# A batch of eight images through pooling branches, depthwise convolutions and attention: borders of the stem's end and of the levels reordered on ScalarE and VectorE, and the box sums of products split into fp32r parts in twelve of 24 steps

## The chip, the cores and the metric

The kernel runs on one core of one Trainium2 chip. A core has five engines that run their own queues in order and meet through semaphores: TensorE (PE, with PEld for its weight loads), VectorE (DVE), ScalarE (ACT), GpSimd (POOL) and SyncE (SP, which issues the DMAs here). The metric is the device time of one execution in microseconds (us), lower is better, as a median of runs.

## The reference

`x` has 8 images of 256 channels and 32x32 pixels. What the change touches lies in the first half of the function, up to the concatenations:

```python
def _sumpool(x): return lax.reduce_window(x, 0.0, lax.add, WIN, (1, 1, 1, 1), PAD)      # 5x5
def _tmaxavg(x): return 0.9 * _maxpool(x) + 0.1 * (_sumpool(x) / 25)
def _rwpool(x):
    c = lax.stop_gradient(jnp.max(x))              # over the whole batch
    e = jnp.exp(x - c)
    return _sumpool(e * x) / (_sumpool(e) + 1e-06)

x_aux = _cbs(_gn(x), w_sta, b_sta)                 # 1x1 convolution to 128 channels, silu
y1, y2 = [x_aux], [x_aux]
for _ in range(3):
    y1.append(_tmaxavg(y1[-1]))
    y2.append(_rwpool(y2[-1]))
y = concat([_cbs(concat(y1), w_cv1, b_cv1), _cbs(concat(y2), w_cv2, b_cv2)])
a = c1(ddwv(ddwh(dwv(dwh(y)))))                    # four depthwise convolutions, one 1x1
x = x + _cbs(y * a, w_cvend, b_cvend)
x = x + attention(_gn(x), w1, w2)                  # 1024 tokens, softmax, per image
```

The maximum `c` of `_rwpool` runs over all eight images, so each of its three applications (a level) needs all images of the one before.

## The kernel before

There are three stages, one after the other, with a barrier of the engines between them: the stem (`phase_a`), the levels (`phase_b`) and the rest, image by image (`phase_c`). The change lies in the first two.

The stem normalises each image on VectorE (`normalise(n)`, two instructions that write `xn`), multiplies by `w_sta` on TensorE (`convolve(n)`), and applies silu on ScalarE (`silu(n)`, into `x_all[:, n, 0]`); VectorE then takes each row's maximum (`maximum(n)`, into `rmc`). ScalarE rounds weights to fp32r (`split`), GpSimd takes the rests (`low_parts`). Beside that, the chain of `_tmaxavg` for image 0 runs in its own tensors (`Chain`): image 0's stem output is loaded into `chain.wide[:, 0]` by a DMA; VectorE forms the 5x5 maximum in seven steps (`chain.maxima(dve, 0, level, steps)`: step 0 writes `pairs`, step 1 is a small copy of borders into `pairs`, 2 writes `work_a`, 3 `tall`, 4 `work_a`, 5 and 6 `work_b`); ScalarE copies the level into `zero` (`chain.zero_level`), and GpSimd forms the 5x5 sum from it in six adds (`chain.box_sum_step`); VectorE joins both into the next level (`chain.mixture_of_sums`). `box` is the 0/1 matrix of neighbouring pixels, rounded once to fp32r from `box_raw`. The orders of these instructions are written out by hand in the code of each engine.

The levels run `_rwpool`. There are 24 steps (`total = LEVELS * B`), numbered m or s: steps 0 to 7 are the images of the first level, 8 to 15 of the second, 16 to 23 of the third. For one step:

- TensorE transposes the image (`turn(m)`, into `ps_t`).
- ScalarE takes the exponential (`exponent(m)`, into `e`) and rounds it to fp32r (`e_hi`). GpSimd takes the rest (`e_low(m)`, `e_lo`). VectorE multiplies (`product(m)`, `ey = e * x`), which frees `ps_t`.
- TensorE sums over 5x5 windows by products with `box`, which also transpose back: `sum_e(m)` as two passes of fp32r matmuls, 10 with `e_hi` and 10 with `e_lo` (`box_sum`), and `sum_ey(m)` in fp32 (`box_sum_whole`), which appears in the trace as 20 matmuls.
- ScalarE forms 1/(sum + eps) by a logarithm and an exponential (`estimate(m)`); VectorE improves it (`residual`, `improve`, into `newton`) and multiplies with the sum of products (`divide(m)`), which gives `y(m)`, back in `x_all`, its row maximum in `rmc`, and frees `ps_ey`. A DMA stores `y(m)`.

At a level's start (s = 0, 8, 16) VectorE and TensorE form the maximum over the batch (`reduce_tile`, `spread_max`, `reduce_batch`), and ScalarE forms `eps` from it (`set_eps`), which `estimate` of that level needs.

In step s TensorE runs sum_ey(s), turn(s + 2), sum_e(s + 1). ScalarE runs estimate(s), exponent(s + 2), and at a level's start the exponent first, then set_eps and estimate. VectorE runs product(s + 1), residual(s), improve(s), divide(s), and then one step of the image 0 chain in some of them. GpSimd runs e_low(s + 2) and then one add of the chain in steps 0 to 5 and 9 to 14. `ps_ey` is a single buffer: sum_ey(s + 1) waits for y(s). `turn` waits for the product before it, since `ps_t` is single too.

## Time and profile before

| | us |
|---|---|
| median of 3 runs | 1458.1 |
| lowest and highest | 1456.68, 1458.79 |
| the profiled execution | 1458.25 |
| its span, first to last instruction | 1456.5 |
| stem, of the span | 0 to about 88.4 |
| levels, of the span | 88.7 to 286.6, then 2.8 for the last store |
| images (`phase_c`) | from 289.5 on |

A page of the profile gives busy times of the engines, the chain of work that ended last, and groups of instructions. The trace behind it gives each instruction with its start. A matmul's end is modelled. Idle time of an engine is shown before the instruction that ended it, with the one it was waiting for.

### The profile page before, as it was taken

The numbers are of one execution on the slowest core, as the hardware profiler recorded it, in microseconds if no ns is written. First come the engines' busy times: TensorE is split into PE (matmuls) and PEld (weight loads), VectorE is DVE, ScalarE is ACT, GpSimd is POOL, SyncE is SP. The second block draws the span as 40 slices with busy tenths as digits, with TensorE's granted clock in tenths as the row PEclk, the third lists the DMA queues.
The fourth block names the chain that finished last, engine by engine and source line by source line (L and its number), as shares of the span: only waits on it lengthen the run. The fifth ranks groups of instructions, "written<-read, shape, count | busy, mean of one in ns | idle before, by whom it ended". The sixth has DMA issues, their size and how long they took to land.

```text
span 1456.5 us, 18340 instructions
## 1 busy us (share of the span) xinstructions
PE 1292.0 (89%) x7162; PEld 1077.5 (74%) x7162; DVE 1143.7 (79%) x1218; ACT 691.9 (48%) x749; POOL 128.8 (9%) x64
## 2 busy tenths in 40 slices
PE   3649898872999999999999999999999999999797
PEld 1238797742768986888688878877986798688597
DVE  7858686678689887988798798879877998796443
ACT  0335564562246536543654365347435653564333
POOL 1645363200000000000000000000000000000000
PEclk9778998985999999999999999999999999999899
DMA  7401122210000020001002000200020002000000
GB/s 286 158 15 73 58 93 82 88 58 0 29 15 1 16 87 14 0 33 68 14 0 72 29 14 0 72 29 14 0 94 6 14 14 86 0 1 30 29 1 29
DMA packets 19175, 62.84 MB, mean 43 GB/s; under 512 B 1600, under 2 KB 4288, under 8 KB 19136
## 3 DMA queue, kind: packets, MB, share of 16 engines
q1 hardware_dynamic: 18432, 62.00, 11.4%
q8 instruction: 27, 0.44, 0.1%
q10 hardware_dynamic: 704, 0.30, 0.1%
q14 instruction: 12, 0.10, 0.0%
HBM read 36.61 MB, written 25.17 MB: 42 GB/s over the span
## 4 chain that ended last, share of the span: by engine, by line
PE 63%; issue 14%; DVE 12%; ACT 5%; DMA 0%; DVEq 0%; ACTq 0%; POOLq 0%; POOL 0%
PE slot L1094 21%; PE slot L1132 12%; PE ps_o L1132 9%; PE ps_ey L565 6%; DVE between L1407 4%; PE slot L549 3%; PE slot L1148 3%; PE ps_e L549 3%; DVE a L1407 2%; PE slot L1072 2%; PE ps_t L633 1%; PE slot L1119 1%; PE ps_ot L1164 1%; ACT f_all L1283 1%; PE slot L1055 1%
## 5 line engine op out<-in xcount | busy, mean ns | idle before, releaser
L1132 PE MATMUL slot<-f_all,q_all 128*128 128x512 f32 x768 | 196.9, 409 | 13.4 <-ACT pooled L1273 13.4
L1132 PE MATMUL ps_o<-v_all,pt_all 128*128 128x256 f32 x1536 | 199.2, 286 | 5.4 <-ACT mixed L1292 5.2
L1132 PEld LDWEIGHTS ps_o<-v_all,pt_all 128*128 128x128 f32 x1536 | 188.8, 192 | 7.6 <-DVE pt_all L1411 6.2
L1132 PEld LDWEIGHTS slot<-f_all,q_all 128*128 128x128 f32 x768 | 145.2, 195 | 43.9 <-ACT pooled L1273 14.8
L1407 DVE SCALAR_TENSOR_TENSOR a<-between,k_columns,a 128x992 f32<-128x992 f32 (+1 forms) x128 | 157.5, 1232 | 4.9 <-ACT a L1264 2.6
L1287 ACT CAST v_all<-y 128x1024 fp32r<-128x1024 f32 x32 | 33.7, 1052 | 185.8 <-DVE y L1438 185.8
L1411 DVE TENSOR_TENSOR pt_all<-slot,pt_all 128x1024 fp32r<-128x1024 f32 x64 | 78.2, 1222 | 47.5 <-ACT pt_all L1278 47.5
L1072 PE MATMUL slot<-wide,k_cv 128*128 128x512 f32 x256 | 114.3, 597 | 0.0
L565 PE MATMUL ps_ey<-box,x_all 128*128 128x192 f32 (+2 forms) x480 | 95.5, 358 | 19.6 <-DVE rmc L751 12.8
L565 PEld LDWEIGHTS ps_ey<-box,x_all 128*128 128x128 f32 x480 | 84.2, 204 | 26.3 <-issue 20.2
L1264 ACT ACTIVATE a<-between,k_columns 128x1024 f32<-128x1024 f32 x64 | 79.5, 1242 | 48.7 <-DVE between L1407 47.7
L1292 ACT ACTIVATE mixed<-ps_o,row_inv 128x256 f32<-128x256 f32 x64 | 30.1, 471 | 151.8 <-PE ps_o L1132 151.8
L1024 POOL TENSOR_TENSOR c_rstd<-c_spread,k_minus_half 128x2 f32<-128x2 f32 x8 | 5.6, 698 | 1093.2 <-DVE gmean L1477 1093.2
L1416 DVE TENSOR_REDUCE c_minus_max<-slot 128x1 f32<-128x1024 f32 x64 | 78.1, 1220 | 11.2 <-PE slot L1132 11.2
L1072 PEld LDWEIGHTS slot<-wide,k_cv 128*128 128x128 f32 x256 | 47.5, 190 | 51.4 <-issue 50.7
L1407 DVE SCALAR_TENSOR_TENSOR between<-y,k_columns,between 128x992 f32<-128x992 f32 x64 | 79.4, 1250 | 7.0 <-ACT between L1264 5.9
L1278 ACT CAST pt_all<-slot 128x1024 fp32r<-128x1024 f32 x64 | 65.0, 1015 | 37.3 <-PE slot L1148 37.1
L1273 ACT ACTIVATE pooled<-slot,c_minus_max 128x1024 f32<-128x1024 f32 x64 | 71.6, 1119 | 21.5 <-DVE c_minus_max L1416 21.5
L1438 DVE SCALAR_TENSOR_TENSOR y<-slot,k_columns,y 128x1024 f32<-128x1024 f32 x32 | 41.0, 1281 | 51.2 <-PE slot L1094 35.0
L1407 DVE SCALAR_TENSOR_TENSOR between<-a,k_columns,between 128x960 f32<-128x960 f32 x64 | 77.2, 1215 | 1.1
L1257 ACT ACTIVATE y<-slot,k_columns 128x1024 f32<-128x1024 f32 x32 | 35.4, 1105 | 81.0 <-PE slot L1094 81.0
L1148 PE MATMUL slot<-k_ident,pooled 128*128 128x128 f32 x512 | 66.8, 273 | 4.0 <-ACT pooled L1273 4.0
(160 smaller groups left out, 2649.3 us busy)
## 6 DMA issues: line engine op xcount, KB each, us to landing
levels<-x_all SPq DMA_DIRECT2D x32, 512.0 KB, 2.6
x_all<-in_x SPq DMA_DIRECT2D x8, 1024.0 KB, 13.2
q_all<-levels SPq DMA_DIRECT2D x8, 1024.0 KB, 4.9
x<-in_x SPq DMA_DIRECT2D x8, 1024.0 KB, 4.8
out<-x SPq DMA_DIRECT2D x8, 1024.0 KB, 3.9
pooled<-levels SPq DMA_DIRECT2D x8, 512.0 KB, 3.3
wide<-levels SPq DMA_DIRECT2D x7, 512.0 KB, 3.3
x_all<-in_w_c SPq DMA_DIRECT2D x2, 512.0 KB, 3.6
```

The lines of the kernel that those rows point to most:

```text
L549: last = nc.tensor.matmul(out[:, r0 * W:r1 * W], part[:, k * P:(k + 1) * P], box[:, c0:c0 + (r1 - r0) * W], start=(b not in started), stop ...
L565: last = nc.tensor.matmul(out[:, r0 * W:r1 * W], whole[:, k * P:(k + 1) * P], box[:, c0:c0 + (r1 - r0) * W].bitcast(F32), start=(b not in ...
L1072: last = nc.tensor.matmul(slot[:, h * HALF:(h + 1) * HALF], keep["cv1"][:, k, cols(m)], rows, start=(k == 0), stop=(k == KT - 1))
L1094: last = nc.tensor.matmul(slot[:, hs], weights[:, k], inputs(k)[:, hs], start=(at == 0), stop=(at == len(uses) - 1))
L1132: last = nc.tensor.matmul(out, lhs, rhs, start=(n == 0), stop=(n == len(parts) - 1))
L1148: last = nc.tensor.transpose(slot[:, cols(m)], prob[:, cols(m)], keep["ident"][:, :])
L1264: nc.scalar.activation(dst, src, ACT.Identity, scale=keep["taps"][:, s, c, 1:2], bias=keep["b_taps"][:, s, c:c + 1]).then_inc(taps_centre. ...
L1273: nc.scalar.activation(prob[:, :], slots_of["s", t][:, :], ACT.Exp, bias=minus_max[:, t:t + 1], accum_out=row_sum[:, t:t + 1]).then_inc(pr ...
L1278: nc.scalar.copy(pt_hi[:, t % 2], slots_of["t", t][:, :]).then_inc(pt_hi_done.sem, 1)
L1407: nc.vector.scalar_tensor_tensor(o, u, keep["taps"][:, s, c, tap:tap + 1], o, ALU.mult, ALU.add).then_inc(taps.sem, 1)
L1411: nc.vector.tensor_tensor(pt_lo[:, t % 2], slots_of["t", t][:, :], pt_hi[:, t % 2].bitcast(F32), ALU.subtract).then_inc(pt_lo_done.sem, 1)
L1416: nc.vector.tensor_reduce(minus_max[:, t:t + 1], slots_of["s", t][:, :], AX, ALU.max, negate=True).then_inc(maxed.sem, 1)
```

## The change

On ScalarE the stem's end runs silu(7), then the rounding of `box` (which VectorE did), and then the copy of level 1 into `zero`; before, that copy, which waits for VectorE's mixture, stood ahead of silu(7).

On VectorE the stem's end runs steps 0 and 1 of the first maxima before maximum(1), normalise(n) before maximum(n - 3), and no step of level 1's maxima; those all move into the levels.

In the levels the sums of products are split: for all steps m outside `WHOLE` (so for 0, 7 to 10 and 17 to 23, twelve steps) ScalarE rounds `ey` to `ey_hi`, GpSimd forms `ey_lo`, and sum_ey is two passes of fp32r matmuls. In 1 to 6 and 11 to 16 it stays fp32. GpSimd's adds for level 2 start one step later (10 to 15); its adds then stand in the steps s in which it forms no `ey_lo`. At a level's start ScalarE runs set_eps and estimate before the exponent. VectorE runs level 1's maxima in steps 0 to 6 (its mixture in 8, before 7) and level 2's in 9 to 14 and 17. The copy of level 2 into `zero` moves from step 8 to 9.

```diff
@@ -403,8 +403,10 @@
             split("c1")
             silu(6)
             split("cv2")
+            silu(7)
+            act.wait_ge(box_in, 16)
+            nc.scalar.copy(box[:, :], box_raw[:, :]).then_inc(box_ready, 1)
             chain.zero_next(act, 1)
-            silu(7)
 
         @block.tensor
         def _(pe):
@@ -519,18 +521,16 @@
             maximum(0)
             shifts(1)
             normalise(group)
+            chain.maxima(dve, 0, 0, 0, 1)
             maximum(1)
-            first_maxima = ((0, 1, 2), (3, 4), (5, 6))
+            between = ((2, 3), (4,), (5, 6))
             for n in range(group + 1, B):
+                normalise(n)
                 maximum(n - 3)
-                normalise(n)
-                chain.maxima(dve, 0, 0, *first_maxima[n - group - 1])
-            dve.wait_ge(box_in, 16)
-            nc.vector.tensor_copy(box[:, :], box_raw[:, :]).then_inc(box_ready, 1)
+                chain.maxima(dve, 0, 0, *between[n - group - 1])
             maximum(B - 3)
             chain.mixture_of_sums(dve, 0)
             maximum(B - 2)
-            chain.maxima(dve, 0, 1, 0, 1, 2)
             maximum(B - 1)
 
 
@@ -569,6 +569,9 @@
     return last
 
 
+WHOLE = frozenset([*range(1, 7), *range(11, 17)])
+
+
 def phase_b(nc, keep, levels, x_all, rmc, box, chain, pooled):
 
 
@@ -585,6 +588,8 @@
         newton = x_all[:, 6, 1]
         e_hi = sb("e_hi", [P, 2, N], F32R)
         e_lo = sb("e_lo", [P, 2, N], F32R)
+        ey_hi = sb("ey_hi", [P, 2, N], F32R)
+        ey_lo = sb("ey_lo", [P, 2, N], F32R)
         tile_max = sb("tile_max", [P, LEVELS])
         batch_max = sb("batch_max", [P, LEVELS])
         minus_max = sb("minus_max", [P, 1])
@@ -596,7 +601,7 @@
 
         turned = sem("turned")
         exp_done, e_hi_done, e_lo_done = sem("exp_done"), sem("e_hi_done"), sem("e_lo_done")
-        ey_done = sem("ey_done")
+        ey_done, ey_hi_done, ey_lo_done = sem("ey_done"), sem("ey_hi_done"), sem("ey_lo_done")
         sum_e_done, sum_ey_done = sem("sum_e_done"), sem("sum_ey_done")
         log_done, r_done = sem("log_done"), sem("r_done")
         residual_done, newton_done, y_done = sem("residual_done"), sem("newton_done"), sem("y_done")
@@ -604,6 +609,10 @@
         shifts_done, eps_set = sem("shifts_done"), sem("eps_set")
         stored = pooled.stored
         block = ctx.enter_context(nc.Block())
+
+        def splits(m):
+
+            return len([k for k in range(m) if k not in WHOLE])
 
         def level_starts(s):
 
@@ -640,10 +649,17 @@
                 box_sum(nc, pe, box, ps_e[:, m % 2], e_hi[:, m % 2], e_lo[:, m % 2], (e_lo_done, m + 1)).then_inc(sum_e_done, 1)
 
             def sum_ey(m):
-                pe.wait_ge(ey_done, m + 1)
+                if m in WHOLE:
+                    pe.wait_ge(ey_done, m + 1)
+                else:
+                    pe.wait_ge(ey_hi_done, splits(m) + 1)
                 if m:
                     pe.wait_ge(y_done, m)
-                box_sum_whole(nc, pe, box, ps_ey, ey[m % 2]).then_inc(sum_ey_done, 1)
+                if m in WHOLE:
+                    last = box_sum_whole(nc, pe, box, ps_ey, ey[m % 2])
+                else:
+                    last = box_sum(nc, pe, box, ps_ey, ey_hi[:, m % 2], ey_lo[:, m % 2], (ey_lo_done, splits(m) + 1))
+                last.then_inc(sum_ey_done, 1)
 
             def spread_max(level):
 
@@ -676,6 +692,12 @@
                 act.wait_ge(exp_done, m + 1)
                 nc.scalar.copy(e_hi[:, u], e[u]).then_inc(e_hi_done, 1)
 
+            def product_hi(m):
+                act.wait_ge(ey_done, m + 1)
+                if m > 1:
+                    act.wait_ge(sum_ey_done, m - 1)
+                nc.scalar.copy(ey_hi[:, m % 2], ey[m % 2]).then_inc(ey_hi_done, 1)
+
             def estimate(m):
                 u = m % 2
                 act.wait_ge(sum_e_done, m + 1)
@@ -698,12 +720,14 @@
                 first = level_starts(s)
                 if s >= 0 and not first:
                     estimate(s)
-                if s + 2 < total:
-                    exponent(s + 2)
+                if 0 <= s + 1 < total and s + 1 not in WHOLE:
+                    product_hi(s + 1)
                 if first:
                     set_eps(s // B)
                     estimate(s)
-                if s == 8:
+                if s + 2 < total:
+                    exponent(s + 2)
+                if s == 9:
                     chain.zero_next(act, 2)
 
         @block.gpsimd
@@ -713,10 +737,17 @@
                 pool.wait_ge(e_hi_done, m + 1)
                 nc.gpsimd.tensor_tensor(e_lo[:, u], e[u], e_hi[:, u].bitcast(F32), ALU.subtract).then_inc(e_lo_done, 1)
 
+            def product_low(m):
+                u = m % 2
+                pool.wait_ge(ey_hi_done, splits(m) + 1)
+                nc.gpsimd.tensor_tensor(ey_lo[:, u], ey[u], ey_hi[:, u].bitcast(F32), ALU.subtract).then_inc(ey_lo_done, 1)
+
             for s in range(-2, total):
+                if 0 <= s + 1 < total and s + 1 not in WHOLE:
+                    product_low(s + 1)
                 if s + 2 < total:
                     e_low(s + 2)
-                for level, begin in ((1, 0), (2, 9)):
+                for level, begin in ((1, 0), (2, 10)):
                     if begin <= s < begin + 6:
                         chain.box_sum_step(pool, 0, level, s - begin)
 
@@ -777,13 +808,14 @@
                     residual(s)
                     improve(s)
                     divide(s)
-                if 0 <= s < 4:
-                    chain.maxima(dve, 0, 1, s + 3)
-                if s == 7:
+                if 0 <= s < 7:
+                    chain.maxima(dve, 0, 1, s)
+                if s == 8:
                     chain.mixture_of_sums(dve, 1)
-                if 9 <= s < 9 + MIX - 1:
+                if 9 <= s < 15:
                     chain.maxima(dve, 0, 2, s - 9)
                 if s == 17:
+                    chain.maxima(dve, 0, 2, 6)
                     chain.mixture_of_sums(dve, 2)
 
 
```

On ScalarE, around step 8, where the second level starts, before: L675 and L677 are the exponent and its rounding, L691 `eps`, L684 and L686 the estimate.

```order
L684 ACTIVATE x_all<-ps_e,eps 128x1024 [waits b_newton_done,b_sum_e_done]
L686 ACTIVATE x_all<-x_all 128x1024 [waits b_log_done]
L675 ACTIVATE x_all<-ps_t,minus_max 128x1024 [waits b_sum_e_done,b_e_lo_done,b_turned]
L677 CAST e_hi<-x_all 128x1024 [waits b_exp_done]
L675 ACTIVATE x_all<-ps_t,minus_max 128x1024 [waits b_sum_e_done,b_e_lo_done,b_turned]
L677 CAST e_hi<-x_all 128x1024 [waits b_exp_done]
L691 ACTIVATE eps<-batch_max,eps_shift 128x1 [waits b_batch_max_done]
L684 ACTIVATE x_all<-ps_e,eps 128x1024 [waits b_newton_done,b_sum_e_done,b_eps_set]
L686 ACTIVATE x_all<-x_all 128x1024 [waits b_log_done]
```

The same place in the changed kernel (L706 and L708 are the estimate, L691 and L693 the exponent, L713 `eps`, L699 the rounding of the product):

```order
L706 ACTIVATE x_all<-ps_e,eps 128x1024 [waits b_newton_done,b_sum_e_done]
L708 ACTIVATE x_all<-x_all 128x1024 [waits b_log_done]
L699 CAST ey_hi<-x_all 128x1024 [waits b_sum_ey_done,b_ey_done]
L691 ACTIVATE x_all<-ps_t,minus_max 128x1024 [waits b_sum_e_done,b_e_lo_done,b_turned]
L693 CAST e_hi<-x_all 128x1024 [waits b_exp_done]
L699 CAST ey_hi<-x_all 128x1024 [waits b_sum_ey_done,b_ey_done]
L713 ACTIVATE eps<-batch_max,eps_shift 128x1 [waits b_batch_max_done]
L706 ACTIVATE x_all<-ps_e,eps 128x1024 [waits b_newton_done,b_sum_e_done,b_eps_set]
L708 ACTIVATE x_all<-x_all 128x1024 [waits b_log_done]
L691 ACTIVATE x_all<-ps_t,minus_max 128x1024 [waits b_sum_e_done,b_e_lo_done,b_turned]
L693 CAST e_hi<-x_all 128x1024 [waits b_exp_done]
```

The exponent of step 10 has moved behind `eps` and the estimate of step 8, and two roundings of `ey` have come in.

On VectorE, step 0 of the levels, before (L735 residual, L742 improve, L751 divide, L730 product):

```order
L735 SCALAR_TENSOR_TENSOR ps_e<-ps_e,eps,x_all 128x1024 [waits b_r_done]
L742 SCALAR_TENSOR_TENSOR x_all<-ps_e,x_all 128x1024 [waits b_residual_done]
L751 ISA x_all,rmc<-x_all,ps_ey 128x1024 [waits stored0,b_sum_ey_done,b_newton_done]
L751 ISA rmc 128x1
L224 TENSOR_TENSOR tall<-work_a,pairs 128x1024 [waits chain_done]
L730 TENSOR_TENSOR x_all<-ps_t,x_all 128x1024 [waits b_sum_ey_done,b_exp_done]
```

and in the changed kernel, with the chain's piece of the next step:

```order
L782 ISA x_all,rmc<-x_all,ps_ey 128x1024 [waits stored0,b_sum_ey_done,b_newton_done]
L782 ISA rmc 128x1
L224 TENSOR_TENSOR pairs<-wide 128x32x31 [waits chain_loaded]
L761 TENSOR_TENSOR x_all<-ps_t,x_all 128x1024 [waits b_sum_ey_done,b_exp_done]
L766 SCALAR_TENSOR_TENSOR ps_e<-ps_e,eps,x_all 128x1024 [waits b_r_done]
L773 SCALAR_TENSOR_TENSOR x_all<-ps_e,x_all 128x1024 [waits b_y_done,b_residual_done]
L782 ISA x_all,rmc<-x_all,ps_ey 128x1024 [waits stored1,b_sum_ey_done,b_newton_done]
L782 ISA rmc 128x1
L203 COPY pairs<-wide 128x32x2
```

Level 1's first three maxima steps, which stood in the stem, now stand behind the divides of steps 0 to 2, and the others three steps later than before.

## Rows read from the trace of the kernel before

**Rows 1.** The page's first line.

```profile
span 1456.5 us, 18340 instructions
```

**Rows 2.** By stretches: busy us (instructions) of PE, PEld, DVE, ACT, POOL; PE clock, DMA, GB/s.

```profile
112.00:119.00 7.00, 6.97 (x25) 6.33 (x26) 4.78 (x5) 0.00 (x0) 0.00 (x0) 0.57 0.18 75
119.00:162.00 43.00, 42.62 (x314) 41.06 (x311) 34.74 (x36) 28.22 (x26) 26.63 (x12) 1.00 0.19 75
290.00:1457.00 1167.00, 1080.38 (x5932) 896.93 (x5932) 936.08 (x989) 567.34 (x629) 5.58 (x8) 0.97 0.08 27
```

**Rows 3.** The chain that ended last, step 6 of the levels: start, us, what.

```profile
148.35 3.50 PE ps_ey L565 x20
151.84 0.87 PE ps_t L633 x8
152.72 2.28 PE ps_e L549 x20
```

**Rows 4.** Timeline of the second level's start: start us, us, engine, line, what [idle before].

```profile
163.46 0.28 DVE L761 TENSOR_REDUCE batch_max<-ps_e 128x1 f32<-128x128 f32 x1
167.33 1.11 ACT L675 ACTIVATE x_all<-ps_t,minus_max 128x1024 f32<-128x1024 f32 x1 [5.74 <-PE ps_t L633]
168.48 1.05 ACT L677 CAST e_hi<-x_all 128x1024 fp32r<-128x1024 f32 x1
169.43 0.29 ACT L691 ACTIVATE eps<-batch_max,eps_shift 128x1 f32<-128x1 f32 x1
169.75 1.11 ACT L684 ACTIVATE x_all<-ps_e,eps 128x1024 f32<-128x1024 f32 x1
175.95 5.43 PE L565 MATMUL ps_ey<-box,x_all 128*128 128x192 f32 x20 [6.38 <-DVE rmc L751]
```

**Rows 5.** Timeline of the first level's start.

```profile
98.84 3.66 PE L565 MATMUL ps_ey<-box,x_all 128*128 128x192 f32 x20
105.69 2.35 POOL L714 TENSOR_TENSOR e_lo<-x_all,e_hi 128x1024 fp32r<-128x1024 f32 x1 [5.09 <-ACT e_hi L677]
108.07 1.29 DVE L735 SCALAR_TENSOR_TENSOR ps_e<-ps_e,eps,x_all 128x1024 f32<-128x1024 f32 x1 [9.72 <-ACT x_all L686]
112.03 6.64 PE L565 MATMUL ps_ey<-box,x_all 128*128 128x192 f32 x20 [6.40 <-DVE rmc L751]
```

**Rows 6.** Timeline, sum_ey of steps 7, 11, 17 and 19, and the last divide.

```profile
154.82 3.66 PE L565 MATMUL ps_ey<-box,x_all 128*128 128x192 f32 x20
...
190.99 3.66 PE L565 MATMUL ps_ey<-box,x_all 128*128 128x192 f32 x20
...
238.52 6.54 PE L565 MATMUL ps_ey<-box,x_all 128*128 128x192 f32 x20 [6.38 <-DVE x_all L754]
...
254.68 3.66 PE L565 MATMUL ps_ey<-box,x_all 128*128 128x192 f32 x20
...
285.36 1.22 DVE L754 SCALAR_TENSOR_TENSOR x_all<-x_all,ps_ey 128x1024 f32<-128x1024 f32 x1
```

**Rows 7.** Timeline of the stem's end, VectorE and GpSimd.

```profile
47.07 1.54 DVE L499 TENSOR_SCALAR xn<-x_all,rstd,shift 128x1024 f32<-128x1024 f32 x2 [0.55 <-PE ps_a L424]
49.71 1.19 DVE L224 TENSOR_TENSOR pairs<-wide 128x992 f32<-128x992 f32 x1 [1.10 <-DMA wide<-x_all]
...
58.58 2.81 POOL L187 TENSOR_TENSOR sum_a<-tall_sum 128x1088 f32<-128x1088 f32 x1
58.97 3.50 DVE L224 TENSOR_TENSOR tall<-work_a,pairs 128x1024 f32<-128x1024 f32 x1
...
75.66 4.58 DVE L529 CAST box<-box_raw 128x256 fp32r<-128x256 f32 x1
80.06 2.39 POOL L454 TENSOR_TENSOR k_cv_lo<-x_all,k_cv_hi 128x1024 fp32r<-128x1024 f32 x1
...
87.19 1.21 DVE L504 TENSOR_REDUCE rmc<-x_all 128x1 f32<-128x1024 f32 x1
```

**Rows 8.** Timeline, the border copy of level 2's maxima in step 10.

```profile
190.52 0.22 DVE L203 COPY pairs<-wide 128x64 f32<-128x64 f32 x1
```

## Prediction, before the changed kernel ran

> **What bounds the kernel now.** I read the span and the busy times by stretches first [rows 1, 2]. In the levels TensorE is busy nearly all the time between 119 and 162 us at full clock, GpSimd two thirds of it; the images from 290 us on take 1167 us and the change touches nothing there. So the change lives in the first 289 us. Then I read the chain that ended last, for a step in the middle of a level [rows 3]: it runs through TensorE alone, 3.50 us of sum_ey, 0.87 of turn, 2.28 of sum_e, 6.65 us a step. At a level's start it leaves TensorE: the timeline shows the batch maximum ready at 163.74, yet ScalarE forms `eps` at 169.43, since it first waits for the transpose of step 10 and runs exponent and rounding (1.11 and 1.05); the estimate starts at 169.75, and TensorE, idle for 6.38 us, starts sum_ey(9) at 175.95 [rows 4]. The same stands at step 1 and at step 17 [rows 5, 6]. From the estimate's start to the next sum_ey it is 175.95 - 169.75 = 6.20 us; I call this the y path. After such an idle time TensorE's clock reads 0.57 for 7 us, near its 1.2 GHz level, and sum_ey takes 6.64 in place of 3.5 [rows 2, 5].
>
> **A split step.** sum_e shows what two fp32r passes cost: 2.28. So a split sum_ey is 2.28 for 3.50, and TensorE's step 2.28 + 0.87 + 2.28 = 5.43. But sum_ey(n+1) also needs y(n), one y path after sum_e(n) ends, and sum_e(n) ends when sum_ey(n) could start at the earliest, 5.43 after sum_ey(n-1) started. Two steps are thus at least 6.20 + 5.43 = 11.6, or 5.8 a step. The split is worth 0.85 a step, not 1.22. ScalarE has five passes of about 1.1 in it (5.4), GpSimd two of 2.35 (4.7) [rows 2, 4, 5]: both fit.
>
> **GpSimd and VectorE exclude each other.** In the stem VectorE's maxima step starts at 58.97, 0.4 after a GpSimd add that ends at 61.39, and ends at 62.47, 1.1 after that end, where such a step alone takes 1.2 [rows 7]. The rounding of `box` started at 75.66 takes 4.58, to just past 80.06, where GpSimd's next instruction starts. So a VectorE instruction with both inputs in SBUF that finds GpSimd at work waits for that instruction's end. In the levels before, none of them met one: the chain's step came just ahead of e_low. When it meets one, product, residual, improve and divide behind it are late.
>
> **The levels, followed through.** I write A(n) for the start of sum_ey(n). A(0) = 98.84 stays.
> - Level 1. `eps` no longer waits for the exponent of step 2, so the estimate starts at 98.9 and A(1) = 105.1, for 112.03 before [rows 5]; the idle time shrinks from 6.4 to under 1 us, and sum_ey(1) runs at full clock. e_low(2) starts at 104.2 (98.84 + 2.28 + 0.87 + 1.15 + 1.05) and ends at 106.6. The maxima step behind divide(0), issued at 105.0, waits for it and ends at 107.7. Product(2) 1.14 more; from a residual's start to the next sum_ey it is 112.03 - 108.07 = 3.96 [rows 5]: A(2) = 112.8. The next chain step is the border copy, 0.22 [rows 8]; if it doesn't wait, y(2) is early again and the rest is TensorE's pace: A(7) = 112.8 + 5 x 6.65 = 146.0, for 154.82 [rows 6]: 8.8 gained.
> - Step 7 gives only half: the last maxima step meets the first `ey_lo` of the level on GpSimd, so A(8) = 153.3.
> - Second start. The batch maximum comes at 154.2, the rounding of the product and `eps` lie in front, the estimate starts at 155.1, A(9) = 161.3, for 175.95: 14.6 gained. The mixture, now in step 8, waits for e_low(10) to 161.7; it ends at 162.8, product 163.9, A(10) = 167.9. The first maxima step of level 2 waits for e_low(11) to 169.9: A(11) = 176.1, for 190.99 [rows 6]: 14.9. Five whole steps and 0.5 for the batch maximum: A(16) = 209.8.
> - Third start: the estimate at 211.3, A(17) = 217.5, for 238.52: 21.0. A(18) = 222.9. In step 17 the last maxima step and the mixture both stand on VectorE, and the mixture waits for e_low(19) to 225.8: 226.9, 228.0, A(19) = 232.0, for 254.68: 22.7.
> - Then 5.8 a step: A(22) = 249.4, sum_e(23) ends at 254.0 (no turn there), and one y path less 0.14 later y(23) at 260.0, for 285.36 + 1.22 = 286.58 [rows 6]: **26.6 gained**. The last store and the start of the images follow it as before.
>
> The 26.6 by cause, roughly: the three starts 6.9, 5.1 and 5.4, the clock that no longer falls there 3.1, 1.8 and 2.9, twelve splits 10, and some 8 to 9 lost again in waits for GpSimd.
>
> **The stem's end, worked at about nothing.** Off VectorE go the rounding of `box` and level 1's first three maxima steps (1.2 + 0.2 + 1.2). Against it, step 0 of level 0's maxima now stands ahead of maximum(1) and normalise(5) and waits for a DMA that lands at 49.7; normalise(5), done at 48.61 before, comes at 52.1 and meets GpSimd twice, to about 56.0 [rows 7]. GpSimd works from 50.9 to 82.45 without a gap, and VectorE's instructions with two inputs take turns with it, so GpSimd's end sets VectorE's: about 82, then the last maxima step, maximum(5), the mixture, maximum(6), maximum(7), 5 x 1.15 and a rest, 88.6 for 88.40. I take +0.2. Bounds: -1, if VectorE is through before GpSimd's last; +2.2, if one instruction more finds GpSimd's long one of 4.5. silu(7) and `box` on ScalarE hide under this.
>
> **Sum.** 1458.25 - 26.6 + 0.2 = 1431.9 against the profiled execution, which lies 0.15 above the median; rounded, **1431.7 us**.
>
> **A rule beside a row.** The border copy of 0.22 has never met GpSimd in the rows of before; the forecast lets it pass. The Trainium skill (SBUF — State Buffer, Who interferes with whom) says that a copy between SBUF tensors can enter a mode that uses the port shared with GpSimd, and then fully waits. No run here shows it for this copy. If so, it speaks for the first rival below.
>
> **Rivals.**
> - *A standing collision.* If the copy, or a shift of 0.5 us, leaves y(n) later than the end of sum_e(n+1), each maxima step meets e_low again, and the lateness feeds itself: a whole step is then e_low 2.35 + maxima 1.1 + product 1.2 + turn 0.87 + sum_e 2.28 = 7.8, for 6.65. Four or five steps in a level, some 5 us: 1437 with one level, 1442 with both. For it: y(1) comes only 0.5 us behind e_low(3)'s start. Against: a copy of 0.22 has room, and TensorE's pace lets y catch up.
> - *The gain at the starts comes back.* The idle times of 2.7 us at step 9 and 3 at step 18 let the clock fall for several us as it did at step 1 (3.1 lost each time), or GpSimd, with 2 x 2.35 and a wait for VectorE, becomes late in split steps, 0.5 each in twelve: 1437 to 1440.
> - *Slower than before.* In split steps TensorE idles 0.4 of 5.8, again and again; if that alone kept it at the lower clock, a step would be about twice 5.4. That is over 5 us a step, and from the sixth such step on the 26.6 are gone; with all twelve, 1470. Against: from 290 us on TensorE is busy for 1080 of 1167 us, 93%, at a granted 0.97 [rows 2].
> - *The stem longer by more than the bound*, through another turn with GpSimd, gives 1434 at +2.2: inside the forecast's range.
>
> **How the numbers follow.** The forecast 0.64 (1428 to 1435: splits at TensorE's own 5.43 would give 1428), the standing collision 0.18, the gain given back 0.12, slower 0.04, and the rest, that both gains cancel, 0.02. The range takes in the forecast and one level and more of collision: 1427 to 1441. A measurement of this kernel tells 0.2%, 2.9 us, from no change. Faster by over that 0.94, the same 0.02, slower 0.04.
>
> **What would show it.** sum_ey(1) 6 to 7 us after sum_ey(0), at a granted clock near 1.00; `eps` ahead of the exponent at 155; split steps 5.8 apart from step 19 on, with TensorE idle for 0.3 to 0.4 on VectorE's y; one long maxima instruction in step 0, at 8, 9 and 17, and none in 2 to 5 and 11 to 14; the border copy at 0.22 and not over 1. Wrong if whole steps are 7.8 apart, if the clock falls at steps 9 or 19, or if the levels start after 91.

## The result, and the profile after

| | before | changed |
|---|---|---|
| median, us | 1458.55 (6 runs, 1456.68 to 1459.97) | 1434.04 (6 runs, 1429.68 to 1436.08) |
| the profiled execution, its span | 1458.25, 1456.5 | 1429.68, 1427.9 |
| levels start (`tile_max`), last `y(23)` ends | 88.72, 286.58 | 87.43, 260.22 |
| first product of the images, from there to the end | 290.71, 1165.8 | 264.30, 1163.6 |

The ratio is 0.983, with an interval of 0.981 to 0.985: 24.5 us less. The forecast was 26.6 - 0.2 less, 1431.7, with a range of 1427 to 1441. The profiled execution happens to be the shortest of the changed kernel's six. In the two profiled executions the levels take 172.8 us in place of 197.9, 25.1 less; the other 3.5 lie ahead of the levels (1.3) and in the images (2.2), whose code the change leaves alone.

The page of the changed kernel, its first line and the granted clock in 40 slices. A slice is 35.7 us; the levels lie in slices 3 to 8.

```profile
span 1427.9 us, 18374 instructions
...
PEclk9879999867999999999999999999999999999899
```

By stretches: the stretch's length, then busy us (instructions) of PE, PEld, DVE, ACT, POOL, then TensorE's granted clock, the DMA engines' share and GB/s.

```profile
98.00:146.00 48.00, 46.44 (x341) 44.35 (x340) 43.50 (x41) 31.72 (x30) 33.95 (x14) 1.00 0.17 69
...
160.00:167.00 7.00, 5.95 (x29) 5.98 (x29) 6.90 (x7) 2.25 (x3) 3.50 (x2) 0.58 0.19 77
167.00:218.00 51.00, 48.57 (x360) 46.86 (x358) 42.11 (x44) 35.79 (x35) 35.13 (x16) 0.99 0.21 83
218.00:223.00 5.00, 4.77 (x29) 4.80 (x29) 4.56 (x5) 2.09 (x2) 3.75 (x2) 0.66 0.27 108
223.00:255.00 32.00, 29.19 (x254) 28.72 (x252) 26.83 (x23) 27.54 (x27) 23.96 (x10) 1.00 0.30 115
```

The first level, which had a stretch at 0.57 [rows 2], now runs at 1.00 from end to end. The clock still falls behind the two later starts, to 0.58 and 0.66. The timeline of the first start (start us, us, engine, line, what, [idle before <- what ended it]):

```profile
97.55 1.31 PE L549 MATMUL ps_ey<-box,ey_hi 128*128 128x192 f32 x10
103.19 2.36 POOL L738 TENSOR_TENSOR e_lo<-x_all,e_hi 128x1024 fp32r<-128x1024 f32 x1 [3.62 <-ACT e_hi L693]
103.79 2.81 DVE L224 TENSOR_TENSOR pairs<-wide 128x992 f32<-128x992 f32 x1
104.01 3.71 PE L565 MATMUL ps_ey<-box,x_all 128*128 128x192 f32 x20 [0.88 <-DVE rmc L782]
...
111.19 2.35 POOL L738 TENSOR_TENSOR e_lo<-x_all,e_hi 128x1024 fp32r<-128x1024 f32 x1 [2.74 <-ACT e_hi L693]
111.37 2.26 DVE L203 COPY pairs<-wide 128x64 f32<-128x64 f32 x1
```

sum_ey(1) comes 6.46 us behind sum_ey(0), where it was 13.19 [rows 5], and TensorE's idle time before it went from 6.40 to 0.88. One maxima step, at 103.79, meets `e_lo` and takes 2.81. And the border copy, at 111.37, takes 2.26 where it took 0.22 [rows 8]: it began 0.18 us after GpSimd's instruction and ended when that had.

The second level's start:

```profile
153.45 0.28 DVE L792 TENSOR_REDUCE batch_max<-ps_e 128x1 f32<-128x128 f32 x1
154.53 0.29 ACT L713 ACTIVATE eps<-batch_max,eps_shift 128x1 f32<-128x1 f32 x1
154.85 1.11 ACT L706 ACTIVATE x_all<-ps_e,eps 128x1024 f32<-128x1024 f32 x1
156.96 1.10 ACT L691 ACTIVATE x_all<-ps_t,minus_max 128x1024 f32<-128x1024 f32 x1
161.05 2.38 PE L549 MATMUL ps_ey<-box,ey_hi 128*128 128x192 f32 x10 [2.71 <-DVE rmc L782]
163.22 2.33 PE L549 MATMUL ps_ey<-box,ey_lo 128*128 128x192 f32 x10
```

`eps` now follows the batch maximum by 1.1 us in place of 6.0 [rows 4], and stands ahead of the exponent. TensorE idles 2.71 us for 6.38, and the two passes behind it run at the lower clock, 2.4 and 2.3 in place of 1.3 each.

The split steps of the third level, and the end:

```profile
225.30 1.31 PE L549 MATMUL ps_ey<-box,ey_hi 128*128 128x192 f32 x10
...
231.69 1.36 PE L549 MATMUL ps_ey<-box,ey_hi 128*128 128x192 f32 x10 [0.80 <-DVE x_all L785]
...
237.17 1.31 PE L549 MATMUL ps_ey<-box,ey_hi 128*128 128x192 f32 x10
...
243.57 1.36 PE L549 MATMUL ps_ey<-box,ey_hi 128*128 128x192 f32 x10 [0.81 <-DVE x_all L785]
...
259.00 1.22 DVE L785 SCALAR_TENSOR_TENSOR x_all<-x_all,ps_ey 128x1024 f32<-128x1024 f32 x1 [0.38 <-PE ps_ey L549]
```

They come 5.48 and 6.40 apart by turns, 5.94 in the mean: every second one waits 0.8 us for y.

### The profile page after: what moved, and what is told of

Same layout as the page of the kernel before. It is cut to its first block, busy times and chain, and to the rows that moved or that the text cites. A ratio compares the mean times of both kernels' runs of the same rounds, so it can differ in the third digit from the quotient of the medians.

```text
span 1427.9 us, 18374 instructions
## 1 busy us (share of the span) xinstructions
PE 1273.4 (89%) x7162; PEld 1063.4 (74%) x7162; DVE 1148.8 (80%) x1217; ACT 704.6 (49%) x762; POOL 159.5 (11%) x76
## 4 chain that ended last, share of the span: by engine, by line
PE 59%; issue 14%; DVE 14%; ACT 6%; DMA 0%; DVEq 0%; ACTq 0%; POOLq 0%; POOL 0%
PE slot L1126 21%; PE slot L1164 12%; PE ps_o L1164 9%; DVE between L1439 5%; PE slot L549 3%; PE slot L1180 3%; DVE a L1439 2%; PE slot L1104 2%; PE ps_e L549 2%; PE ps_ey L565 2%; PE slot L1151 1%; PE ps_ey L549 1%; DVE ps_e L766 1%; DVE x_all L773 1%; PE ps_t L642 1%
## 5 line engine op out<-in xcount | busy, mean ns | idle before, releaser
L1296 ACT ACTIVATE a<-between,k_columns 128x1024 f32<-128x1024 f32 x64 | 79.4, 1241 | 48.6 <-DVE between L1439 47.7
L738 POOL TENSOR_TENSOR e_lo<-x_all,e_hi 128x1024 fp32r<-128x1024 f32 x24 | 61.5, 2563 | 47.6 <-ACT e_hi L693 47.6
L1126 PE MATMUL slot<-f_all,k_c_hi 128*128 128x512 f32 x232 | 64.0, 397 | 2.5 <-DVE y L1470 2.5
```

Of the source, the lines that this page charges most:

```text
L738: nc.gpsimd.tensor_tensor(e_lo[:, u], e[u], e_hi[:, u].bitcast(F32), ALU.subtract).then_inc(e_lo_done, 1)
L1126: last = nc.tensor.matmul(slot[:, hs], weights[:, k], inputs(k)[:, hs], start=(at == 0), stop=(at == len(uses) - 1))
L1296: nc.scalar.activation(dst, src, ACT.Identity, scale=keep["taps"][:, s, c, 1:2], bias=keep["b_taps"][:, s, c:c + 1]).then_inc(taps_centre. ...
```

## Experiments

The theory after this result: nearly all of the gain is ScalarE's new order at the three starts, with those falls of the clock that it avoids. The splits and the moved chain nearly cancel, since each place where the chain meets GpSimd costs what some two splits give. The rival: the parts give what the forecast's sum put down for each, above all 10 us for twelve splits. Each run below stands beside runs of the kernel before on the same chip; the medians of those were 1458.76 to 1458.97. "Levels" is from `tile_max` to the end of `y(23)` in the profiled execution, "images" from the first product behind it to the end of the span.

| kernel | median (lowest, highest) | ratio, interval | levels | images |
|---|---|---|---|---|
| before | 1458.55 (1456.68, 1459.97) | | 197.9 | 1165.8 |
| changed | 1434.04 (1429.68, 1436.08) | 0.983, 0.981 to 0.985 | 172.8 | 1163.6 |
| e1_again | 1433.90 (1431.58, 1439.19) | 0.983, 0.981 to 0.984 | 175.9 | 1168.6 |
| e2_no_split | 1435.62 (1432.99, 1436.68) | 0.984, 0.982 to 0.985 | 173.7 | 1167.2 |
| e3_splits_only | 1455.68 (1451.00, 1461.56) | 0.998, 0.997 to 1.000 | 194.9 | 1164.9 |
| e4_tail | 1435.45 (1435.07, 1438.07) | 0.985, 0.983 to 0.986 | 172.7 | 1167.7 |
| e5_act_order | 1436.49 (1431.40, 1437.74) | 0.984, 0.982 to 0.985 | 175.2 | 1167.4 |
| e6_border_reduce | 1433.64 (1432.82, 1441.62) | 0.984, 0.982 to 0.987 | 172.9 | 1164.9 |
| e7_placed_a | 1425.14 (1424.34, 1426.96) | 0.977, 0.976 to 0.978 | 163.5 | 1167.0 |
| e8_placed_b | 1428.43 (1428.08, 1428.56) | 0.979, 0.978 to 0.980 | 164.7 | 1168.7 |
| e9_old_stem | 1435.92 (1430.51, 1441.38) | 0.984, 0.982 to 0.986 | 173.7 | 1163.8 |
| e10_placed_whole | 1432.96 (1430.84, 1437.16) | 0.983, 0.980 to 0.985 | 171.1 | 1165.6 |

**e1_again**, the changed kernel once more, no edit.

> The changed kernel again, unaltered, for a second profile and more times: its six times spread over 6.4 us, those of before over 3.3. Theory A (clock): the waits for y at steps 9, 17 and 23 let TensorE's clock fall in some executions and not in others; the levels then end between 257 and 263 us after the span's start, whole steps stay 6.6 apart, and where the end is late a granted clock near 0.6 stands behind one of those waits. Theory B (standing collision): in slow executions the maxima steps of level 1 or 2 meet e_low again and again, whole steps are 7.8 apart, and several maxima rows take over 2 us. Time 1430 to 1437.

The median is the same, but the profiled execution, the longest of its five, is 9.5 us longer: 3.1 in the levels, 5.0 in the images, 1.2 before the levels. Theory A had the late end come with a fall of the clock. It was the other way round: the levels end at 264.5, beyond Theory A's 263, in the execution in which the clock at step 17 did not fall. So `e_lo` came early enough to meet the mixture, which in the first execution it had missed (there the last maxima step at 223.22 and the mixture at 224.55 took 1.22 each). Timeline of step 17:

```profile
225.15 2.39 POOL L738 TENSOR_TENSOR e_lo<-x_all,e_hi 128x1024 fp32r<-128x1024 f32 x1 [1.16 <-ACT e_hi L693]
225.40 3.22 DVE L230 SCALAR_TENSOR_TENSOR wide<-sum_b,work_b 128x1024 f32<-128x1024 f32 x1
...
230.03 1.06 PE L642 MATMUL ps_t<-k_ident,x_all 128*128 128x128 f32 x8 [2.65 <-DVE x_all L761]
...
234.86 2.33 PE L549 MATMUL ps_ey<-box,ey_hi 128*128 128x192 f32 x10
```

The mixture takes 3.22, TensorE idles 2.65 and then has the lower clock; sum_ey(19) starts 9.9 us behind sum_ey(18) where it was 6.4. Whole steps stay 6.63 apart in both executions, so there is no standing collision. The images differ mostly in the last one. From its `f_all` (ScalarE's first rounding of `pooled` for it) to the end the stretches read, first of the changed kernel's first profile, then of this one,

```profile
1201.42:1427.90 226.48, 203.52 (x1174) 172.91 (x1172) 138.16 (x162) 102.65 (x121) 1.39 (x2) 0.98 0.04 16
```

```profile
1206.89:1437.40 230.51, 207.56 (x1174) 176.74 (x1172) 138.28 (x162) 102.65 (x121) 1.39 (x2) 0.95 0.04 16
```

The same 1174 matmuls take 226.5 us at a granted 0.98 and 230.5 at 0.95. The other 1.0 us of the images lies ahead of them.

**e2_no_split**, the changed kernel with every sum of products in fp32:

```diff
-WHOLE = frozenset([*range(1, 7), *range(11, 17)])
+WHOLE = frozenset(range(24))
```

> All of the change except the splits: sum_ey is fp32 in all 24 steps; the orders of ScalarE and VectorE and the later chain stay. By the recurrence of the prediction with this kernel's order: the starts gain as before, steps go at 6.65, the mixture and maxima steps meet e_low as in the changed kernel: the levels end 24 us earlier than before, 1434 to 1436, about 3 us over the changed kernel. Rival (splits carry their 10 us in full on top of the orders): 1441 or more.

1.6 us more than the changed kernel, within both runs' scatter, and not 10. By levels, from the traces: first level (sum_ey(0) to sum_ey(8)) 53.3 us against 55.1 with the splits, second 57.4 against 57.3, third (to the end of `y(23)`) 52.7 against 50.2. So in these two executions the splits gain 2.5 us in the third level and lose 1.8 in the first; e1's third level, with its collision, took 53.2, and there they gain nothing. In step 0 a split cannot help, since y(0) waits for the estimate anyway; but it brings `e_lo` of step 2 forward by 1.2 us, into the chain's first maxima step. Without it that step took 1.19 and the border copy behind it 0.23. In the second level the chain's instructions of steps 8 to 10 met `e_lo` in whole steps too (3.02, 3.30 and 2.33). The mixture's new place does that: in e5 below, with whole steps and the mixture still in step 7, the same three took 1.22, 1.19 and 0.22.

**e3_splits_only**, the kernel before with the twelve splits and nothing else (of the edit, `WHOLE` and ScalarE's order; the rest of the splits' code is as in the change):

```diff
+WHOLE = frozenset([*range(1, 7), *range(11, 17)])
...
-                if s + 2 < total:
-                    exponent(s + 2)
+                if 0 <= s + 1 < total and s + 1 not in WHOLE:
+                    product_hi(s + 1)
+                if s + 2 < total:
+                    exponent(s + 2)
                 if first:
                     set_eps(s // B)
                     estimate(s)
```

> The kernel before with the twelve splits alone: stem, level starts on ScalarE (exponent ahead of eps) and VectorE's chain as before. If the splits are worth 0.85 each and the y path (6.2) is the limit of a split step: the levels end about 12 us earlier, 1446, split steps 5.8 to 6.2 apart, idle times of 6 us at steps 1, 9 and 17 stay, with the clock falling behind them. If splits are worth 1.22 each: 1443 or less. If they are worth nothing alone, 1456 or more.

A miss: 3.3 us gained against the kernel before on the same chip. The mixture of level 1 stood behind step 7's divide, and with step 7 split it met `e_lo`. Timeline:

```profile
159.71 2.33 POOL L738 TENSOR_TENSOR e_lo<-x_all,e_hi 128x1024 fp32r<-128x1024 f32 x1
160.11 3.02 DVE L230 SCALAR_TENSOR_TENSOR wide<-sum_b,work_b 128x1024 f32<-128x1024 f32 x1
163.17 0.16 DVE L788 TENSOR_REDUCE tile_max<-rmc 128x1 f32<-128x8 f32 x1
163.38 0.69 PE L667 MATMUL ps_e<-k_ident,tile_max 128*128 128x128 f32 x2 [3.85 <-DVE tile_max L788]
...
177.25 2.42 PE L549 MATMUL ps_ey<-box,ey_hi 128*128 128x192 f32 x10 [6.40 <-DVE rmc L782]
```

The mixture's 3.02 holds `tile_max` back and TensorE idles 3.85 there, with a granted clock of 0.66 over the 5 us behind it, ahead of the old 6.40 which stays. The level's two splits were eaten at its end: it took 64.6 us for 63.9 before. The second level, with three splits, took 63.1 for 62.6; its border copy met `e_lo` (1.93). Only the third, whose seven splits meet no instruction of the chain but the mixture, at 1.22, gained: 56.0 for 61.2, 0.7 us a split.

**e4_tail**, the changed kernel with the last maxima step and the mixture of level 2 behind the last divide:

```diff
-                if s == 17:
+                if s == total - 1:
                     chain.maxima(dve, 0, 2, 6)
                     chain.mixture_of_sums(dve, 2)
```

> The changed kernel with the last maxima step and the mixture of level 2 moved from step 17 behind the last divide (step 23). In step 17 they cost the wait for GpSimd and two instructions, 3 us by the prediction's recurrence, and behind the last divide VectorE is idle while the last store lands (2.8 us), so they should cost nothing there: 3 us less than the changed kernel, sum_ey(19) 6 us after sum_ey(18) in place of 8.6 to 9.1. Rival: the time comes back because the end of the levels waits for VectorE (2.4 us of work, ends within 0.5 us of the store): no gain or 0.5.

No gain in the median. In the profiled execution the clock fell at step 17 (the two passes of sum_ey(17) took 1.46 and 2.33), as in the changed kernel's first profile, and sum_ey(19) comes 6.4 us after sum_ey(18) in both: where the clock falls there was no collision to take away, and the levels are as long, 172.7 against 172.8. The two instructions behind the last divide end 2.5 us after it, at 263.7, yet the images' first product comes 4.4 us behind `y(23)`, for 4.1 to 4.4 in the kernels without them: they are nearly hidden. Whether an execution in which the clock stays up would be 3 us shorter than e1's levels stays open; none was profiled. The rest of the median is the images' 1167.7.

**e5_act_order**, the kernel before with ScalarE's order at a level's start alone:

```diff
-                if s + 2 < total:
-                    exponent(s + 2)
                 if first:
                     set_eps(s // B)
                     estimate(s)
+                if s + 2 < total:
+                    exponent(s + 2)
```

> The kernel before with one part of the change alone: at the two places where a level begins, ScalarE takes set_eps, the logarithm and the reciprocal before the exponential and copy of the step after next. The pooling chain, the whole-product sums (all 24) and the stem stay as before. Theory A: this order is nearly the whole gain. TensorE's idle 6.40 us at the two starts goes, the clock stays up behind it, and steps 8 and 16 to 17 come 7.9 and 7.3 us apart: sum_ey(1) at 105.2, sum_ey(9) at 160.3, sum_ey(17) at 215.3, the end of y(23) at 260.4, levels 171.8 long against 197.9 before; median 1431 to 1437 us. Theory B: the chain of before, whose last maximum and mixture stand at steps 3 and 7, meets the earlier start (as the splits alone did, where the mixture held the first divide of the level back), so half of the gain is lost: an idle of over 3 us of TensorE at one of the starts, levels of 180 to 186 us, median 1442 to 1448.

This swap gives 22.3 of the changed kernel's 24.5 us, and the intervals of the two overlap. It is 0.9 us over e2, which has the swap, the new stem and the moved chain: within both runs' scatter. The levels took 175.2 us, 3.4 over Theory A's 171.8; some 2 of it lie at the first start, where sum_ey(0) itself ran at a granted 0.63 (98 to 104 us) and sum_ey(1) came 8.27 behind it. The old chain did not get in the way:

```profile
153.42 1.22 DVE L230 SCALAR_TENSOR_TENSOR wide<-sum_b,work_b 128x1024 f32<-128x1024 f32 x1
154.10 2.75 POOL L714 TENSOR_TENSOR e_lo<-x_all,e_hi 128x1024 fp32r<-128x1024 f32 x1 [4.27 <-ACT e_hi L677]
...
156.21 0.29 ACT L691 ACTIVATE eps<-batch_max,eps_shift 128x1 f32<-128x1 f32 x1 [2.19 <-DVE batch_max L761]
```

In whole steps the chain's instruction starts 0.7 us ahead of `e_lo` and runs free, as it did before. The idle time before sum_ey(9) is 0.75, and from 104 to 225 us the granted clock reads 1.00. It reads 1.00 there in e2 and e10 too, the other kernels with the swap and without splits; in the seven profiles with the swap and splits it reads 0.96 to 0.99.

**e6_border_reduce**, the changed kernel with the 64 border elements written by another instruction:

```diff
-                own.did(self.nc.vector.tensor_copy(pairs[:, :, 1:W + 2:W], src[:, :, 0:W:W - 1]))
+                own.did(self.nc.vector.reduce_max(pairs[:, :, 1:W + 2:W],
+                        src[:, :, 0:W:W - 1].rearrange("p h (w o) -> p h w o", o=1), AX))
```

> The changed kernel with the pooling chain's border columns (64 elements) written by a reduction over an axis of length 1 in the place of the copy. Theory A: the copy waited for GpSimd (2.26 and 1.50 us where it had taken 0.22) because of the form of the instruction, a copy between SBUF tensors; a reduction with one input does not wait: 0.2 to 0.3 us at steps 1 and 10, whatever GpSimd runs. Theory B: whatever reads and writes SBUF at that moment waits: 1.4 to 2.3 us again. On the whole kernel both give the changed kernel's time within 1.5 us by A (one wait of up to 2.0 us is gone at step 1, where sum_ey(2) came 7.6 behind sum_ey(1), so at most 1 us of it shows at each of two steps): 1431.5 to 1434.5.

```profile
113.04 2.36 POOL L738 TENSOR_TENSOR e_lo<-x_all,e_hi 128x1024 fp32r<-128x1024 f32 x1 [2.73 <-ACT e_hi L693]
...
113.22 0.27 DVE L203 TENSOR_REDUCE pairs<-wide 128x64 f32<-128x64 f32 x1
```

At the same place, 0.18 us behind GpSimd's start, the reduction takes 0.27; the copy took 2.26. Over its 24 places it took 0.26 to 0.27. The Trainium skill (SBUF — State Buffer, "Who interferes with whom") says that a copy can enter a mode in which it needs the pair of ports shared with GpSimd and waits in full for GpSimd to finish, and that on this chip a reduction never contends; both halves agree with these rows, 2.26 and 0.27. The kernel's time does not show it: the step behind it was sum_ey(3), only 0.4 us late with the copy.

**e7_placed_a** and **e8_placed_b**, the changed kernel with the chain placed step by step. The places come from carrying the forecast's recurrence (each start of a sum worked out from those before it) through all 24 steps for many placements. A pair (level, k) is maxima step k, 7 the mixture; EARLY is ahead of the step's residual, LATE behind its divide. The edit of e7, in part:

```diff
-WHOLE = frozenset([*range(1, 7), *range(11, 17)])
+WHOLE = frozenset([4, 5, 6, 7, 8, 10, 16, 17])
+EARLY = {0: ((1, 0),), 1: ((1, 1),), 8: ((1, 7),), 16: ((2, 3),), 23: ((2, 6),)}
+LATE = {1: ((1, 2),), 3: ((1, 3),), 4: ((1, 4),), 5: ((1, 5),), 6: ((1, 6),), 9: ((2, 0),),
+        10: ((2, 1), (2, 2)), 19: ((2, 4),), 21: ((2, 5),), 23: ((2, 7),)}
...
-                if s == 9:
+                if s == 11:
                     chain.zero_next(act, 2)
-                for level, begin in ((1, 0), (2, 10)):
+                for level, begin in ((1, 0), (2, 12)):
...
+                pooling(EARLY.get(s, ()))
                 if s >= 0:
                     residual(s)
                     improve(s)
                     divide(s)
-                if 0 <= s < 7:
-                    chain.maxima(dve, 0, 1, s)
...
+                pooling(LATE.get(s, ()))
```

> The changed kernel with the pooling chain placed step by step where the recurrence that was worked out from the rows finds room: level 1's maxima behind steps 0 (before its residual), 1 (before), 1, 3, 4, 5, 6, its mixture before step 8's residual; level 2's behind 9, 10, 10, 16, 19, 21, 23; GpSimd's second chain from step 12; whole products only for 4 to 8, 10, 16, 17, so that 16 steps are split. No work is left out. Theory A (the waits between GpSimd and VectorE and the whole products' 6.63 us a step are what the levels still lose): sum_ey(9) at 157.6, sum_ey(17) at 207.0, y(23) ends at 248.5 against 260.2 to 264.5, 12 to 16 us less: median 1418 to 1424. Theory B (GpSimd, busy 2 x 2.33 us a split step besides its chain, falls behind, and each collision of 2 us drops the clock): gaps over 1.4 us at three steps or more, y(23) ends after 258, median 1430 to 1436.

> As the kernel before this one, with another placement: level 1's first three operations ahead of step 0's residual, then behind steps 1, 3, 4, 6 and 7; level 2's from the start of step 8 on, its last maximum and mixture behind step 23; ScalarE at a level's start takes the logarithm and reciprocal ahead of the copy of the product; whole products for 0, 4, 5, 7, 16, 17 only (18 splits). No work is left out. Theory A: sum_ey(9) at 158.0, sum_ey(17) at 208.0, y(23) ends at 249.7, the chain's tail 2.3 us after it is covered; median 1419 to 1426. Theory B (with 18 splits GpSimd is the bound: 2 x 2.33 + 2.3 of the chain is 7 us in each step that has all three): steps of 7 us wherever GpSimd's chain runs, y(23) ends after 258, median 1430 to 1438.

Both beat the changed kernel: e7 by 8.9 us, 0.6%, with intervals that don't touch. Both lie a little above the range that was put down for them, by 1.1 and 2.4 us. e7's levels take 163.5 us. The longest collision is not gone there but stands where nothing waits behind it (three shorter ones, of 1.54 to 2.20 us, stay elsewhere):

```profile
150.95 2.36 POOL L742 TENSOR_TENSOR e_lo<-x_all,e_hi 128x1024 fp32r<-128x1024 f32 x1 [3.87 <-ACT e_hi L697]
...
151.80 2.58 DVE L230 SCALAR_TENSOR_TENSOR wide<-sum_b,work_b 128x1024 f32<-128x1024 f32 x1
...
155.31 1.29 DVE L770 SCALAR_TENSOR_TENSOR ps_e<-ps_e,eps,x_all 128x1024 f32<-128x1024 f32 x1 [0.93 <-ACT x_all L712]
```

The mixture waits for `e_lo`, but VectorE's next instruction waits 0.93 longer for ScalarE's estimate anyway. e8 puts more of the chain into the starts, splits eighteen steps in place of sixteen, and lets ScalarE round the product behind `eps` and the estimate at a start. That last part shows: sum_ey(9) comes 7.61 behind sum_ey(8), for 8.36 in the changed kernel, where the rounding (1.05) stands ahead of `eps`, and 7.47 in e2, which has none. Its profiled execution is 4.3 us longer than e7's, 1.2 of it in the levels (chain instructions at 204.66 and 211.07 took 2.45 and 2.98), 0.9 before them, 0.5 from `y(23)` to the first product and 1.7 in the images.

**e9_old_stem**, the changed kernel with the stem's old order on ScalarE and VectorE (in part):

```diff
-            silu(7)
-            act.wait_ge(box_in, 16)
-            nc.scalar.copy(box[:, :], box_raw[:, :]).then_inc(box_ready, 1)
             chain.zero_next(act, 1)
+            silu(7)
-            chain.maxima(dve, 0, 0, 0, 1)
-            between = ((2, 3), (4,), (5, 6))
+            first_maxima = ((0, 1, 2), (3, 4), (5, 6))
...
```

> The changed kernel with the order of the stem's end as it was before on ScalarE and VectorE (gate of level 1 opened ahead of the last two SiLUs, box copied on VectorE, maxima of level 0 in threes behind the normalisations); only the three maxima of level 1, which the changed kernel takes among the level steps, stay out of it. Theory A: the stem's edits are worth nothing: the profiles with the new stem had tile_max at 87.43 to 89.01, those with the old one at 87.85 to 88.72, so it comes at 87.4 to 89.0 here, and the median is the changed kernel's within 1 us, 1433 to 1436. Theory B: the new order shortens the stem by 0.8 to 1.3 us (88.72 against 87.43 in the first pair of profiles): median 1435 to 1437, tile_max at 88.5 or later.

`tile_max` at 87.94, in the middle of the other profiles (87.43 to 89.01), and a median 1.9 us over the changed kernel's, with runs from 1430.51 to 1441.38 on both sides of it. A difference is not shown: by the traces it is within the 1.6 us over which `tile_max` scatters, and the medians alone can't tell 2 us here.

**e10_placed_whole**, e7 with `WHOLE = frozenset(range(24))`.

> The kernel of e7_placed_a with all 24 sums of products whole (GpSimd subtracts nothing for them). Theory A: the splits are worth 1.2 us each only where the pooling chain keeps out of GpSimd's and VectorE's way, as it does in this placement: without the 16 splits steps are 6.63 apart, sum_ey(9) at 159.2, sum_ey(17) at 213.4, y(23) ends near 258.5 to 261 against 251.6 of e7; median 1431 to 1435, 7 to 10 us over e7's 1425.1. Theory B: the gain of e7 is that of the chain's place, and the splits add as little as in the changed kernel (1.6 us): y(23) ends before 255, median 1425 to 1428.

7.8 us over e7: in this placement sixteen splits are worth 7.6 us of the levels in the traces, half a microsecond each, against 1.6 for twelve in the changed kernel. Of it 3.9 lie in the second level and 3.1 in the third. With whole steps the placement itself gives 1432.96, 2.7 less than e2, its counterpart with the changed kernel's chain; the two intervals overlap.

## The prediction, point by point

**What bounds the kernel, and the starts: right.** TensorE's chain in a whole step is 6.63 us, as forecast; the idle times of 6.4 us were ScalarE's order. e5 shows that this alone is 22.3 us; the forecast's terms for it, 6.9, 5.1 and 5.4 for the starts and 3.1, 1.8 and 2.9 for the clock, add up to 25.2.

**The times of the steps: the end right to 1.5 us in 161, single steps up to 3.7 off.** From sum_ey(0), forecast and measured:

| | sum_ey(1) | (2) | (7) | (8) | (9) | (10) | (11) | (16) | (17) | (18) | (19) | (22) | y(23) ends |
|---|---|---|---|---|---|---|---|---|---|---|---|---|---|
| forecast | 6.3 | 14.0 | 47.2 | 54.5 | 62.5 | 69.1 | 77.3 | 111.0 | 118.7 | 124.1 | 133.2 | 150.6 | 161.2 |
| changed | 6.5 | 14.1 | 47.7 | 55.1 | 63.5 | 72.2 | 79.0 | 112.5 | 120.7 | 127.8 | 134.1 | 151.5 | 162.7 |

Two errors stand out, and both are of one kind. At steps 9 and 17 the clock fell, 2.1 and 1.7 us lost (sum_ey(10), sum_ey(18)); the forecast had the idle time at step 9 (2.7, measured 2.71) but gave the fall to a rival, and had named a fall at step 9 or 19 as a sign of being wrong. That sign came. That the end is right all the same is in part luck: the loss was partly made up, because what came late then met no collision: the maxima step behind divide(9) took 1.19 at 167.56 and the mixture of step 17 1.22, both forecast as waiting for `e_lo`. e1 shows the other branch of the second: no fall, but the wait, and the same loss or more. The clock's course at a start also varies with the same code: in e6 and e9, equal to the changed kernel there but for the border copy and the stem, sum_ey(10) came 7.06 and 7.07 behind sum_ey(9) in place of 8.69, but sum_ey(12) came 8.4 behind sum_ey(11), after an idle time of 1.6, and the second level took 57.8 for 57.3.

**The cost of a split step: right in kind, 0.14 us short.** Two steps were to be one y path and one step of TensorE's own, 5.8 in the mean; they are 6.40 and 5.48, 5.94. The y path itself was right: ScalarE's estimate of step 18 started at 225.50 and sum_ey(19) at 231.69, 6.19 later. What the sum put at nothing is the 0.20 from sum_ey(18), at 225.30, to that estimate; TensorE's own step was 5.48 for 5.43.

```profile
225.50 1.12 ACT L706 ACTIVATE x_all<-ps_e,eps 128x1024 f32<-128x1024 f32 x1
```

**The sum by cause: the split's 10 and the waits' 8 to 9 hold as a pair only.** Their difference, 1 to 2, agrees with e2's 1.6, which is itself within the runs' scatter. As separate terms they were book-keeping: without splits there are fewer waits to pay (none in the first level), so removing the splits gives the waits back. e3's expectation took the splits by themselves, at 12 us, and missed by 9. A term of a sum that comes with its own counter-term can't be carried to another kernel alone.

**GpSimd and VectorE exclude each other: right**, and seen at every place where a two-input instruction of the chain started while GpSimd ran `e_lo` or `ey_lo`: 2.81, 2.59, 1.83 in the changed kernel, 3.22 in e1, 3.02 in e3. The forecast's steps did not use the other direction, which the changed kernel shows too: an `e_lo` started at 118.50, 0.11 us behind a maxima step of 1.22, took 3.34 in place of 2.35.

**The border copy: wrong.** The forecast let it pass at 0.22; it took 2.26 and, in step 10, 1.50. The step that failed is the reading of a row in which the two engines had not met as if it told what happens when they do, against the rule of the Trainium skill (SBUF — State Buffer, "Who interferes with whom"), which was named. A row that the forecast did use spoke against it as well: the rounding of `box`, a copy with one input, took 4.58 beside a GpSimd instruction that ended at 80.09,

```profile
74.62 5.47 POOL L454 TENSOR_TENSOR k_c_lo<-x_all,k_c_hi 128x2048 fp32r<-128x2048 f32 x1
```

and on ScalarE the same rounding took 0.40 in the changed kernel. The copy's wait was worth little: sum_ey(3) came 7.02 behind sum_ey(2), 0.4 over a whole step, so no standing collision followed, since TensorE's pace lets y catch up, the reason that the forecast gave: the next steps are 6.69 and 6.63 apart.

**The stem, +0.2: within its bounds.** `normalise(5)` came at 51.08 and took 3.69, `tile_max` at 87.43 to 89.01 over the profiles with the new order and at 87.85 to 88.72 over those with the old one. The -1.3 of the first pair of profiles is thus not shown to be the change's: there the first maxima step, which waits for the DMA of image 0, started 1.0 us earlier already, at 48.72 against 49.71.

**The images: not in the forecast.** It took them as fixed. They take 1163.6 to 1168.7 us over the profiles without regard to the kernel. The last image, from its `f_all` on, takes 226.4 to 226.6 us in four profiles (granted 0.98; before, changed, e9, e10), 228.7 to 228.9 in three (0.96; e2, e3, e6) and 230.4 to 230.5 in five (0.95); the seven before it take 936.1 to 939.2, and why those scatter stays open. The spread of 5 us is as large as the differences between the changed kernel and e1, e2, e4 to e6 and e9, which is why only e3, e7, e8 and e10 are told apart from their neighbours here, and of these e10 only from e7.

## What to carry to other kernels

At a place where one engine's program order holds a short chain of dependent work behind a long independent piece, swap the two first and measure that alone: here the swap was nine tenths of the whole change's gain. A saving on the bounding engine that moves another engine's work forward should be followed to the shared resource it will now hit; the split steps paid only once the maxima stood clear of GpSimd's instructions or where VectorE had to wait anyway. And a duration read where two engines did not meet is a lower bound, not a price.

## What the runs showed of the hardware

- A copy of 64 strided fp32 elements between SBUF tensors on VectorE waits for a GpSimd instruction to end (2.26 us beside one of 2.35); a reduction over an axis of length 1 that writes the same elements does not (0.27).
- The same idle time of TensorE, 1.43 us at step 17, was followed by a granted clock of 0.66 over 5 us in one execution (two passes of 1.62 and 2.33) and by none in the next (1.36 and 1.31), with the same code; in e4, e6 and e9 it was followed by the fall. One of 2.71 at step 9 was followed by the fall in both, one of 1.39 in e7 by passes of 1.75 and 2.34 (its step 23).
- A fall of the clock can cost nothing more than itself, or even less, when it delays an instruction past a collision: the changed kernel's third level is 3.0 us shorter in the execution whose clock fell there (50.2 against 53.2; in e6 and e9, where it fell there too, 50.0 and 50.1).
- The last image took one of three times, whatever the kernel: 226.5 us at a granted 0.98, 228.8 at 0.96 or 230.5 at 0.95, each within 0.1, for the same 1174 matmuls.
- The wait between VectorE and GpSimd goes both ways: a GpSimd instruction of 2.35 that starts 0.1 us behind a two-input instruction of VectorE (1.22) takes 3.34.
